# A fused attention and mixture-of-experts kernel: norms finished on ScalarE, two weighted value rows on ScalarE and added on GpSimd, an input load placed last in the DMA queue's step

## What is computed

```python
x = x + xattn(ctx, ctx, layernorm(x))       # x: 4096 x 512, ctx: 3202 x 512, one head, softmax over all 3202 keys
x = x + ffn(layernorm(x))                   # 16 experts, top 2, capacity 512 rows each, hidden 256
def xattn(k, v, q):
    probs = softmax((q Wq^T + bq)(k Wk^T)^T / sqrt(512))
    return (probs (v Wv^T + bv)) Wo^T + bo
```

## Time and profile before

| what | value |
|---|---|
| median of the 3 timed runs | 1792.59 us |
| the profiled execution, its own time | 1790.13 us |
| its span, first to last instruction | 1788.4 us |
| mean granted TensorE clock | 0.951 of full |

### The profile page before, as it was taken

How to read it: one execution, slowest core, us unless ns; L and a number is a source line. 1 busy time by engine, 2 the same in 40 slices (tenths; PEclk the granted TensorE clock), 3 DMA queues, 4 the chain that set the end, 5 groups by cost and what they waited for, 6 DMA issues and landing times. The chain is left out here.

```text
span 1788.4 us, 40760 instructions
## 1 busy us (share of the span) xinstructions
PE 1611.5 (90%) x15565; PEld 1058.9 (59%) x15565; DVE 1248.5 (70%) x2427; ACT 589.9 (33%) x902; POOL 744.9 (42%) x708
## 2 busy tenths in 40 slices
PE   8999989899998999999999899998998369999974
PEld 4444867667766667666776666776665135555430
DVE  4443277888888888888888888888888365555524
ACT  2343233233232332323323233232332025454430
POOL 0100054355443454434544345444455245665540
PEclk9999999999999999999999999999999679999985
DMA  4310112332223322233222322223221268989969
GB/s 153 90 48 7 55 29 66 62 53 47 49 69 59 59 47 47 68 62 59 47 48 70 59 58 47 47 65 64 55 45 37 43 187 186 218 202 217 199 86 375
DMA packets 339922, 155.75 MB, mean 87 GB/s; under 512 B 268642, under 2 KB 285026, under 8 KB 339876
## 3 DMA queue, kind: packets, MB, share of 16 engines
q1 hardware_dynamic: 317424, 111.05, 25.8%
q0 software_dynamic: 16896, 35.42, 10.4%
q10 hardware_dynamic: 5556, 8.66, 1.3%
HBM read 95.04 MB, written 60.06 MB: 87 GB/s over the span
## 5 line engine op out<-in xcount | busy, mean ns | idle before, releaser
L45 PE MATMUL sc<-qt,kT 128*128 128x128 f16 x3100 | 524.5, 219 | 3.8 <-POOL before L821 3.4
L46 PE MATMUL sc<-qt,kT 128*128 128x128 f16 x3100 | 524.4, 219 | 0.0
L47 PE MATMUL sc<-qt,kT 128*128 128x128 f16 x3100 | 524.3, 219 | 0.0
L45 PE MATMUL acc<-vv,pT 128*128 128x512 f16 x800 | 312.7, 391 | 14.3 <-DVE pT L1025 7.8
L46 PE MATMUL acc<-vv,pT 128*128 128x512 f16 x800 | 312.6, 391 | 0.0
L47 PE MATMUL acc<-vv,pT 128*128 128x512 f16 x800 | 312.0, 390 | 0.0
L45 PEld LDWEIGHTS sc<-qt,kT 128*128 128x128 f16 x3100 | 303.6, 98 | 10.4 <-POOL before L821 3.9
L46 PEld LDWEIGHTS sc<-qt,kT 128*128 128x128 f16 x3100 | 303.7, 98 | 3.5
L47 PEld LDWEIGHTS sc<-qt,kT 128*128 128x128 f16 x3100 | 303.7, 98 | 0.0
L858 POOL TENSOR_TENSOR sum<-s_T 128x512 f32<-128x512 f32 x32 | 72.7, 2273 | 378.7 <-ACT s_T L910 378.7
L858 POOL TENSOR_TENSOR sum<-sum,s_T 128x512 f32<-128x512 f32 (+1 forms) x160 | 209.5, 1309 | 31.5 <-issue 16.8
(11 more groups left out here) (292 smaller groups left out, 2849.7 us busy)
## 6 DMA issues: line engine op xcount, KB each, us to landing
xq<-in_x_dram SPq DMA_DIRECT2D x32, 256.0 KB, 2.9
x_in<-in_x_dram SPq DMA_DIRECT2D x32, 256.0 KB, 2.8
raw_g<-in_L_ffn_w_gate_dram SPq DMA_DIRECT2D x16, 512.0 KB
raw_f<-in_L_ffn_w_fc_dram SPq DMA_DIRECT2D x16, 512.0 KB
raw_p<-in_L_ffn_w_proj_dram SPq DMA_DIRECT2D x16, 512.0 KB
y_dram<-x SPq DMA_DIRECT2D x32, 256.0 KB
rows_dram<-row SPq DMA_DIRECT2D x32, 256.0 KB
blocks_r<-row_bl SPq DMA_DIRECT2D x32, 256.0 KB, 2.0
```

Source lines behind the costliest of these rows:

```text
L45: pe.matmul(out, s_hi, m_hi, start=first, stop=False)
L46: pe.matmul(out, s_hi, m_lo, start=False, stop=False)
L47: return pe.matmul(out, s_lo, m_hi, start=False, stop=last)
```

## The change

Four things are done to `attend`.

1. The two tail keys' values are no longer multiplied and added by VectorE in `residual`. VectorE writes `p_rel` = tail probabilities times 1/sum at the end of `inverse(t)`; ScalarE multiplies the two value rows with it (`tail_values(t)`, two instructions, before `tail_exp(t+1)`), and GpSimd adds both to `xb` in `add_bias(t)`, which has three 128x512 additions in a row instead of one. `add_bias(t)` moves from behind `deviation(t-1)` to the end of GpSimd's step, behind `sums(t+1)`.
2. The router rows' norm moves from VectorE (`normed`, removed) to ScalarE, as two instructions in `rows_high`: minus the mean (`neg_mean`, a new small VectorE instruction), then times `rstd`.
3. The query's norm moves from VectorE (L1135, L1137) to ScalarE, at the start of `query_high`; `shift_q` is now made on GpSimd with two more small instructions in `deviation_q`.
4. `load_x(t+1)` with its wait on `xb` moves from the first to the last place of the SP queue's step.

```diff
                 def step(t, post, more_x, more_q, turn_q):
-                    if more_x:
-                        sp.wait_ge(xb_rdy, t + 1)
-                        load_x(t + 1)
                     if post:
...
                         turn_query(t + 2)
+                    if more_x:
+                        sp.wait_ge(xb_rdy, t + 1)
+                        load_x(t + 1)
 
...
                     wait_for(pool, x1_rdy, t)
-                    pool.tensor_tensor(xb[:], x_in[:], bo_row[:], ALU.add).then_inc(xb_rdy, 1)
+                    pool.tensor_tensor(xb[:], x_in[:], bo_row[:], ALU.add)
+                    for i in range(TAIL):
+                        pool.drain()
+                        pool.wait_ge(vr_rdy, TAIL * t + i + 1)
+                        added = pool.tensor_tensor(xb[:], xb[:], v_rel[:, i, :], ALU.add)
+                    added.then_inc(xb_rdy, 1)
 
...
                     pool.wait_ge(q_var, t - 1)
-                    pool.tensor_tensor(rstd_q[:], var_q[:], nhalf[:], ALU.pow).then_inc(q_rstd, 1)
+                    pool.tensor_tensor(rstd_q[:], var_q[:], nhalf[:], ALU.pow)
+                    pool.drain()
+                    pool.tensor_tensor(mr_q[:], mv_q[:, 0:1], rstd_q[:], ALU.mult)
+                    pool.drain()
+                    pool.tensor_tensor(shift_q[:], ones_f[:, 0:1], mr_q[:], ALU.subtract).then_inc(q_rstd, 1)
 
...
                         deviation(t - 1)
-                        add_bias(t)
                     if post and placed:
...
                         sums(t + 1, 1 - h)
-
-                add_bias(0)
+                    add_bias(t)
+
                 sums(0, 0)
...
                 def rows_high(t):
+                    act.wait_ge(mv_rdy, t + 1)
+                    wait_for(act, rb_rdy, t)
+                    act.activation(xs2[:], x1[:], ACT.Identity, bias=neg_mean[:]).then_inc(xs_rdy, 1)
                     act.wait_ge(xs_rdy, t + 1)
+                    act.wait_ge(rs_rdy, t + 1)
                     wait_for(act, r_out, 16 * t)
-                    wait_for(act, rb_rdy, t)
-                    act.activation(row16[:, 0:D], xs2[:], ACT.Copy, scale=XN_S).then_inc(xs_hi, 1)
+                    act.activation(row16[:, 0:D], xs2[:], ACT.Copy, scale=rstd[:]).then_inc(xs_hi, 1)
+
+                def tail_values(t):
+                    act.wait_ge(rinv_rdy, t + 1)
+                    wait_for(act, xb_rdy, t)
+                    for i in range(TAIL):
+                        act.activation(v_rel[:, i, :], v_tail[:, i, :], ACT.Copy, scale=p_rel[:, i:i + 1]).then_inc(vr_rdy, 1)
 
...
                 def query_high(t):
+                    act.wait_ge(q_rstd, t - 1)
+                    wait_for(act, qb_rdy, t - 2)
+                    act.activation(xqs[:], xq[:], ACT.Identity, bias=shift_q[:], scale=rstd_q[:]).then_inc(q_xs, 1)
                     act.wait_ge(q_xs, t - 1)
-                    wait_for(act, qb_rdy, t - 2)
                     act.activation(q16[:, 0:D], xqs[:], ACT.Copy, scale=XN_S).then_inc(q_hi, 1)
...
                         rows_high(t - 1)
+                        tail_values(t)
                     if more:
+                        tail_values(t)
                         tail_exp(t + 1)
...
                     dve.tensor_tensor(rs_v[:], p_tail[:, 0:1], p_tail[:, 1:2], ALU.add)
-                    dve.tensor_copy(p_held[:], p_tail[:])
                     dve.drain()
...
                     dve.drain()
-                    dve.reciprocal(rinv[:], rs_v[:]).then_inc(rinv_rdy, 1)
+                    dve.reciprocal(rinv[:], rs_v[:])
+                    dve.drain()
+                    wait_for(dve, vr_rdy, TAIL * t)
+                    dve.tensor_scalar(p_rel[:], p_tail[:], rinv[:], None, ALU.mult).then_inc(rinv_rdy, 1)
 
...
                     wait_for(dve, x1_out, 16 * t)
-                    for i in range(TAIL):
-                        dve.scalar_tensor_tensor(out=x1[:], in0=v_tail[:, i, :], scalar=p_held[:, i:i + 1],
-                                                 in1=x1[:] if i else acc[:], op0=ALU.mult, op1=ALU.add)
-                        dve.drain()
-                    dve.scalar_tensor_tensor(out=x1[:], in0=x1[:], scalar=rinv[:], in1=xb[:],
+                    wait_for(dve, xs_rdy, t)
+                    dve.scalar_tensor_tensor(out=x1[:], in0=acc[:], scalar=rinv[:], in1=xb[:],
                                              op0=ALU.mult, op1=ALU.add).then_inc(x1_rdy, 1)
...
                     dve.drain()
-                    dve.tensor_scalar(var_e[:], mv[:, 1:2], EPS, None, ALU.add).then_inc(mv_rdy, 1)
-
-                def normed(t):
-                    dve.wait_ge(rs_rdy, t + 1)
-                    dve.tensor_scalar(xs2[:], x1[:], mv[:, 0:1], rstd[:], ALU.subtract, ALU.mult).then_inc(xs_rdy, 1)
+                    dve.tensor_scalar(neg_mean[:], mv[:, 0:1], -1.0, None, ALU.mult)
+                    dve.tensor_scalar(var_e[:], mv[:, 1:2], EPS, XN_S ** -2, ALU.add, ALU.mult).then_inc(mv_rdy, 1)
 
...
                     dve.wait_ge(xs_hi, t + 1)
-                    dve.scalar_tensor_tensor(out=row16[:, D:2 * D], in0=xs2[:], scalar=XN_S, in1=row16[:, 0:D],
+                    dve.scalar_tensor_tensor(out=row16[:, D:2 * D], in0=xs2[:], scalar=rstd[:], in1=row16[:, 0:D],
                                              op0=ALU.mult, op1=ALU.subtract).then_inc(xs_lo, 1)
...
                     if c == 3:
+                        wait_for(dve, q_xs, t - 2)
                         dve.wait_ge(q_ld, 16 * (t - 1))
...
                         dve.tensor_scalar(var_q[:], mv_q[:, 1:2], EPS, None, ALU.add).then_inc(q_var, 1)
-                    if c == 4:
-                        dve.wait_ge(q_rstd, t - 1)
-                        dve.tensor_scalar(shift_q[:], mv_q[:, 0:1], rstd_q[:], 1.0, ALU.mult, ALU.subtract)
-                        dve.drain()
-                        dve.tensor_scalar(xqs[:], xq[:], rstd_q[:], shift_q[:], ALU.mult, ALU.subtract).then_inc(q_xs, 1)
                     if c == 5:
...
                         if c == 2 and post:
-                            normed(t - 1)
-                            rows_low(t - 1)
+                                rows_low(t - 1)
                         if c == 3 and post:
...
                         place(t - 2)
-                        normed(t - 1)
                         rows_low(t - 1)
...
                 residual(NT - 1)
-                normed(NT - 1)
                 rows_low(NT - 1)
```

More of the change, by code:

```diff
@@ L634, in attend @@
         p_tail = buf("p_tail", [P, TAIL], F32)
-        p_held = buf("p_held", [P, TAIL], F32)
+        p_rel = buf("p_rel", [P, TAIL], F32)
+        v_rel = buf("v_rel", [P, TAIL, D], F32)
+        neg_mean = buf("neg_mean", [P, 1], F32)
+        mr_q = buf("mr_q", [P, 1], F32)
         sum4 = buf("sum4", [P, CH, P], F32)
@@ L699, in attend @@
         qb_rdy, qb_out = sem("qb_rdy"), sem("qb_out")
-        rinv_rdy = sem("rinv_rdy")
+        rinv_rdy, vr_rdy = sem("rinv_rdy"), sem("vr_rdy")
         x_ld = sem("x_ld")
```

## The result

The changed kernel takes 1911.4 us (median of 4, 1910.48 to 1913.07); the kernel before, beside it, 1791.45. The ratio is 1.067 with a 95% interval of 1.0652 to 1.0689: slower by 6.7%, +120 us. The sign was forecast, the size was not: the forecast was 1844, the range ended at 1876.

A forecast was written before the change was run, and what follows sets the result against it. VectorE was taken to bound the loop at 37.46 us a tile. 20.16 + 15.75 + 2.58 = 38.5, with 0.75 for the clock 39.25: +50 over 28 tiles, +4 at the ends, 1844 us, range 1812 to 1876.

The forecast's parts named there:

- What bounds the kernel: Attention loop: VectorE is the bound at 37.46 us a tile; TensorE with no wait would take about 34.6.
- GpSimd's three additions: Behind the sums: 1.27 us each, 4.26 in all with gaps; VectorE stalls 4.76 us a tile at `residual`.
- M to R: From the broadcast of the greatest score (L1016) to `residual`'s start: 20.16 us a tile instead of 15.40.
- R3: VectorE's wait at `residual`: GpSimd's additions come in time and TensorE bounds; 1710 us, chance 0.07.
- R to L: From the start of `residual` to VectorE's last maximum (L1006): 15.75 us a tile instead of 18.86.
- `residual`, `place` and `normed`: VectorE's work after `residual` starts: -1.64, -0.8 and -1.37 us a tile.
- The query's norm: Chain from the query's variance (L1132) to the maximum of chunk 5: 3.37 us, +0.43 a tile (bounds -0.3, +0.9).
- The clock: TensorE's low level after a 4 us wait, in three tiles of four: mean cost 0.75 us a tile.
- L to M: From the last maximum (L1006) to the next broadcast: 2.58 us at full TensorE clock, 3.60 at low.
- R2: Low TensorE clock in every tile, additions at 1.41 us: 40.2 us a tile, 1871 us; chance 0.13.
- The sum: Loop: 39.25 us a tile against 37.46, +50 over 28 tiles, +4 for first and last tiles: +54.
- The table load: ScalarE's norms each bring two loads: 2.6 us a tile more, 1917 us; 0.05 with other large losses.

The follow-up runs named there:

- adds_split: Changed kernel with GpSimd's order `deviation_q`, first addition, scatter, other two additions, sums: 1713.0 us, 0.9566 of the kernel before.
- one_add: Changed kernel with GpSimd's second and third addition cut from 512 columns to 1: 1833.0 us, 1.0237 of the kernel before.
- adds_before_sums: Changed kernel with `add_bias(t)`, all three additions, ahead of `sums(t+1)` on GpSimd: 1738.4 us, 0.9699 of the kernel before.
- row_norm_back: Changed kernel with the router rows' norm back on VectorE: 1894.5 us, 1.0565 of the kernel before.
- qdev_first: Changed kernel with `deviation_q(t+2)`, the query's power, ahead of `scatter(t-2)` on GpSimd: 1870.2 us, 1.0436 of the kernel before.
- tensor_filled_24: Changed kernel with 24 matmuls nobody reads ahead of TensorE's transpose: 1889.2 us, 1.0532 of the kernel before.

## Why the prediction was right and wrong

- **What bounds the kernel** held. VectorE's chain was the bound, in the changed kernel with a stall for GpSimd in it. TensorE's floor of about 34.6 us a tile was never reached: adds_split takes 34.8, and TensorE still waits 0.5 of it.
- **GpSimd's three additions** held: M to R 20.13 for 20.16, an addition 1.27 for 1.27. That it is only 0.03 off is partly luck: in the tile shown the sums end 0.15 us earlier after M than the prediction had it (15.65 for 15.80), and `residual` follows the last addition by 0.27 where it had 0.1. `one_add` shows that they are in the ring at their length, `adds_before_sums` that their place is the cause. Rival R3, the faster one, describes another kernel: the 4.8 us that it asked for are found if the additions go ahead of the sums, and then the time is 1738. Its 1710 is nearly met, at 1713, only with two other repairs, since its 15.75 from R to L isn't met in either.
- **`residual`, `place` and `normed`** held as terms: from R to the query's variance 9.22, against 8.99 by the same terms. L1126 takes 0.16 as forecast. But `row_norm_back` shows that a term which held gained nothing: the time went into the next wait. `tail_values` cost nothing, as forecast: its rows end at 655.32, and ScalarE then waits 0.90 us for VectorE before `tail_exp`.
- **The query's norm** is the step that failed. "The new chain: GpSimd begins 0.23 after L1132" took the distance from the kernel before. There GpSimd had finished its scatter before the variance came, by 0.98 us in the tile read the earlier trace rows and by 1.2 on average (as rows 2):

```profile
POOL rstd_q L850 <- DVE var_q L1132: 33.1, 28, 1.5
```

I never asked what stood ahead of the power in GpSimd's list. The prediction's own terms moved L1132 3.7 us forward. They moved the scatter, which waits for `place`, forward by less, since the 1.37 of `normed` lie between the two; that alone is more than the 1.2. The scatter also became 0.7 us longer (5.49 for 4.75, means of the tiles). Two of its small instructions take 0.72 each where they took 0.18 and 0.20; they now run beside VectorE's L1083 and L1023 and end with them. GpSimd before, GpSimd after, VectorE after:

```profile
642.31 0.18 POOL L839 COPY tok<-P 128x2 f32 x1
642.63 0.20 POOL L841 CAST idx<-idf 128x2 int32<-128x2 f32 x1
```

```profile
642.40 0.72 POOL L847 COPY tok<-P 128x2 f32 x1
643.25 0.72 POOL L849 CAST idx<-idf 128x2 int32<-128x2 f32 x1
```

```profile
642.33 0.75 DVE L1083 SCALAR_TENSOR_TENSOR row<-xs,rstdb,row 128x512 f16<-128x512 f32 x1
643.24 0.69 DVE L1023 TENSOR_TENSOR rm<-rm,s_T 128x512 f32<-128x512 f32 x1 [0.16 <-issue]
```

1.4 and 0.7 less the slack of 1.2 are the 0.9 us by which the power is late. Measured against the forecast: the power's start 1.17 for 0.23, the gap ahead of `mr_q` 0.74 for 0.14, ScalarE's pass 0.81 for 0.63. That is +1.72, and from variance to the maximum 5.06 for 3.37 (the terms as written add up to 3.39), +1.69. 28 tiles: 47 us. `qdev_first` gives back 41 by moving that one wait. Against the kernel before it is +2.1, and the prediction's bound of +0.9 was too near for the same reason.
- **The clock** was mis-sized. The prediction had L to M at 3.33, the low level in three tiles of four, R2 in each; it came in each, 3.8. That is 0.48 x 28 = 13 us, and `tensor_filled_24` prices the level as a whole at 1.24 us a tile. TensorE waited 5.9 us instead of the 4 forecast. Where it waits 3.9, in `row_norm_back`, L to M is 3.38; where it waits 4.4, in `qdev_first`, 3.74. So the price was about right for a wait of 4 us, and the wait was mis-sized; the longer query chain is only part of that, since in `qdev_first`, without it, most of the 0.48 is still there.
- **The sum**: 0.03 less, 2.01 and 0.48 more a tile are 69 us; with the 54 forecast, 123, for 120 measured. The extra 4 us for the first and last tiles didn't come (+1.4 and -0.4).
- **The table load** (R5, 1917) comes near the measured time and is wrong: the profile after has the same single load of the setup and none in the loop. The time alone would have spoken for it.
- **`load_x`** cost nothing, as forecast. It passes thirteen issues, not ten: three stores, `load_xq`, and nine block transfers.

## What to carry to other kernels

Where each engine has a fixed list, an instruction's price is that of its place: ask what stands ahead of it in its list at the time at which it will be asked for, not at which it was. When one edit makes an engine faster, redo each distance behind it that ends in another engine's list; a slack of 1 us between two engines (here 1.2 on average) is a bound on what may be gained, and beyond it the gain turns into a wait. Work moved to an idle engine goes into its idle time only if its inputs are ready then: here they were ready 3.1 us before the broadcast (655.32 for 658.39), so 5.9 us before the sums start, which is room for the three additions' 4.2 us, and the changed order didn't use it.

## What the runs showed of the hardware

- Matmuls whose result nobody reads can pay. With 24 of them in a wait of 6 us the granted clock stayed at 1.00 and the tile became 1.3 us shorter; with 18 it fell in 11 of 24 tiles.
- A one-column sum on VectorE took 1.81 us (0.15 alone) while GpSimd added 128x512, and ended with it. It goes the other way too: in adds_split VectorE's three subtractions run beside GpSimd's last addition and its first sum, and take 5.79 us instead of 3.63, the addition 2.02 instead of 1.27. VectorE's timeline:

```profile
664.38 5.79 DVE L1046 TENSOR_TENSOR s_T<-s_T,m_b 128x1024 f32<-128x1024 f32 x3
```

and GpSimd's:

```profile
664.71 2.02 POOL L836 TENSOR_TENSOR xb<-xb,v_rel 128x512 f32<-128x512 f32 x1 [0.20 <-issue]
666.87 2.09 POOL L872 TENSOR_TENSOR sum<-s_T 128x512 f32<-128x512 f32 x1
```

The Trainium skill, page GPSIMD Engine Reference, section 8 Key points, says that GpSimd shares its SBUF interfaces with VectorE and contends with VectorE instructions that have two SBUF inputs. The traces agree.
- A ScalarE pass over 128x512 took 0.63 us with a constant scale, 0.72 with a bias or a scale from a tensor, 0.81 with both (ScalarE's groups of the changed kernel by shape, 300 to 1400 us, columns as in rows 6):

```profile
L956 ACT ACTIVATE xqs<-xq,shift_q,rstd_q 128x512 f32<-128x512 f32 x27 | 21.9, 812 | 206.7 <-POOL shift_q L862 206.7
L935 ACT ACTIVATE xs<-x,neg_mean 128x512 f32<-128x512 f32 x27 | 19.5, 723 | 99.4 <-DVE var_eb L1079 99.4
L939 ACT ACTIVATE row<-xs,rstdb 128x512 f16<-128x512 f32 x27 | 19.5, 722 | 3.1
```

- GpSimd had 0.74 us between a power and the small product behind it when two indirect transfers came just before, 0.33 when 1 us of idle time lay between, and 0.14 where the scatter stood behind the power. What it does in that time isn't known from these runs.
